# One MoE layer on one core: all expert low halves cut on VectorE, three shared units held back instead of two

## The reference

```python
x = x + jnp.tanh(g_xattn[0]) * attention(layernorm(x), ctx_1024, mask, W, b)
hidden = layernorm(x)
logits = hidden @ w_router
top_logits, top_idx = jax.lax.top_k(logits, 2)
scores = jax.nn.softmax(top_logits, axis=-1)
for e in range(8):                      # every token through its two experts
    proj, gate = jnp.split(rows_of_e @ fc1_w[e], 2, axis=-1)
    out_of_e = jax.nn.silu(proj) * gate @ fc2_w[e]
shared = jax.nn.silu(hidden @ gate_w) * (hidden @ up_w) @ down_w
x = x + jnp.tanh(g_ffn[0]) * (sum_of_two_experts_by_scores + shared)
```

## Time and profile before

| | |
|---|---|
| median of 3 runs | 239.54 us (239.11 to 240.22) |
| the profiled execution | 239.18 us |
| its span in the trace | 237.4 us |
| PE busy | 221.6 us, 93% |
| DVE busy | 173.8 us, 73% |
| ACT busy | 130.0 us, 55% |
| POOL busy | 125.4 us, 53% |
| PE's clock granted | 0.997 of full speed |

### The profile page before, as it was taken

One profiled execution on the slowest core, in us unless ns is written; L12 is line 12 of the kernel. 1 busy time (PEld: TensorE's weight loads), 2 busy tenths in 40 slices (PEclk: granted clock), 3 DMA queues, 4 the chain that ended last, 5 costly groups with the idle time before them and its releaser, 6 DMA issues.

```text
span 237.4 us, 5269 instructions
## 1 busy us (share of the span) xinstructions
PE 221.6 (93%) x1417; PEld 193.4 (81%) x1417; DVE 173.8 (73%) x514; ACT 130.0 (55%) x316; POOL 125.4 (53%) x177
## 2 busy tenths in 40 slices
PE   7988999999899999999599999999999999999980
PEld 7778899978688888888488888888888888887860
DVE  1978797797668899999967656656656656655895
ACT  2556888772647644555126556556556556555320
POOL 1698997564777877887601344344344343343600
PEclk9999999999999999999999999999999999999998
DMA  4899940000122215322242533433433432109777
GB/s 157 269 394 404 405 184 0 0 3 22 45 94 77 80 70 203 133 71 93 76 127 67 145 105 91 120 105 93 115 103 89 123 90 68 49 29 305 260 233 303
DMA packets 18131, 32.05 MB, mean 135 GB/s; under 512 B 3046, under 2 KB 9323, under 8 KB 18104
## 3 DMA queue, kind: packets, MB, share of 16 engines
q1 hardware_dynamic: 14096, 22.28, 29.6%
q0 software_dynamic: 3408, 8.46, 9.6%
q10 hardware_dynamic: 600, 0.97, 1.1%
HBM read 19.95 MB, written 12.67 MB: 137 GB/s over the span
## 4 chain that ended last, share of the span: by engine, by line
PE 45%; POOL 8%; issue 6%; DVE 3%; DMA 2%; ACT 0%; SPq 0%; DVEq 0%; POOLq 0%
PE bank L987 38%; POOL rows L388 6%; PE bank L1232 4%; PE bank L1252 4%; POOL ew_lo L243 2%; DVE acc L959 1%; DMA rows<-hrows,slot 1%; DMA hrows<-rows 1%; DVE act_lo L630 1%; DVE acc L702 1%; SPq L280 0%; DVE act L922 0%; ACT act_hi L443 0%; ACT act L581 0%; DVEq L62 0%
## 5 line engine op out<-in xcount | busy, mean ns | idle before, releaser
L430 POOL DMA_INDIRECT parts<-y_out,dst x39 | 38.8, 995 | 69.7 <-DVE dst L916 66.0
L922 DVE TENSOR_TENSOR act<-act,bank 128x256 f32<-128x256 f32 x39 | 16.4, 421 | 34.4 <-ACT act L581 32.6
L388 POOL DMA_INDIRECT rows<-hrows,slot x32 | 35.1, 1097 | 12.3 <-issue 12.1
L581 ACT ACTIVATE act<-bank 128x256 f32<-128x256 f32 x39 | 15.0, 384 | 37.5 <-PE bank L987 37.5
L987 PE MATMUL bank<-ew_hi,m_xt_hi 128*128 x78 | 30.9, 396 | 0.1
L987 PE MATMUL bank<-ew_hi,m_xt_lo 128*128 x78 | 30.8, 395 | 0.0
L987 PE MATMUL bank<-ew_lo,m_xt_hi 128*128 x78 | 30.7, 394 | 0.0
L987 PE MATMUL bank<-ew_hi,act_hi 128*128 x78 | 25.2, 323 | 0.2 <-DVE act_lo L630 0.2
L443 ACT ACTIVATE act_hi<-act 128x512 fp32r<-128x512 f32 x16 | 10.1, 631 | 21.8 <-DVE act L689 21.8
L987 PE MATMUL bank<-ew_hi,act_lo 128*128 x78 | 21.9, 281 | 0.0
L987 PE MATMUL bank<-ew_lo,act_hi 128*128 x78 | 21.9, 281 | 0.0
(11 more groups left out here) (182 smaller groups left out, 656.8 us busy)
## 6 DMA issues: line engine op xcount, KB each, us to landing
ew_raw<-in_chunks SPq DMA_DIRECT2D x12, 512.0 KB, 10.7
hrows<-rows SPq DMA_DIRECT2D x39, 130.0 KB, 2.3
low_buf<-parts SPq DMA_DIRECT2D x4, 512.0 KB, 4.2
high_buf<-parts SPq DMA_DIRECT2D x4, 512.0 KB, 5.1
acc<-in_x SPq DMA_DIRECT2D x7, 256.0 KB, 5.7
sw_raw<-in_chunks SPq DMA_DIRECT2D x3, 512.0 KB, 8.4
out<-acc SPq DMA_DIRECT2D x3, 512.0 KB, 3.4
rows<-pad_rows SPq DMA_DIRECT2D x9, 130.0 KB, 2.5
```

Source lines behind the costliest of these rows:

```text
L388: pool.indirect_dma_start(out=rows, out_offset=bass.IndirectOffsetOnAxis(ap=slot[:, h, k, i:i + 1], axis=0), in_=hrows[:, HT * h + i, :], ...
L430: pool.indirect_dma_start(out=parts, out_offset=bass.IndirectOffsetOnAxis(ap=dst[:, t:t + 1], axis=0), in_=y_out[:, t % SLOTS, :], in_offs ...
L581: a.activation(act[:, p, 0:I], M_H[p][:, 0:I], ACT.Silu).then_inc(s["m_sil"], 1)
L922: TT(act[:, p, 0:I], act[:, p, 0:I], M_H[p][:, I:2 * I], ALU.mult).then_inc(s["m_prod"], 1)
```

## The change

- All 23 low halves behind the first 7 are cut by DVE, by a new table `LATER` (1 with unit 0, 3 with unit 2, and so on up to 2 ahead of the product of unit 12). `MID` and `LAST` are gone, and POOL runs its scatters without cuts between or behind them.
- `HELD` is 3: the gate, up, product and down of unit 13 move behind the tiles. DVE's order in the tail has the third unit's `product` and `product_lo` between its high adds.
- ACT cuts four high halves earlier (ahead of `norm_second(6)`), one fewer in units 4 and 5 each, and none in a unit 12 of the loop, which is the last before the tiles now; the wait for the end of the attention (`mt_ps`) moves to chunk 12 (`FREE`).
- As the last unit ahead of the tiles is 12 in place of 13, the PSUM banks of the tile stage (`M_H`, `M_A`, `M_X`) are exchanged in pairs.

```diff
--- before.py
+++ after.py
@@ -44,11 +44,10 @@
 NH = 2
 HT = NT // NH
 IN_A = 7
-HELD = 2
+HELD = 3
 U0 = UNITS - HELD
-MID = tuple(IN_A + 2 * i for i in range(5))
-LAST = tuple(range(CHUNKS - 3, CHUNKS))
-LATER = {3: 1, 4: 1, 5: 1, 6: 1, 7: 1, 8: 1, 9: 2, 10: 2, 11: 2, 12: 3}
+FREE = SCH + 6
+LATER = {0: 1, 1: 0, 2: 3, 3: 1, 4: 2, 5: 1, 6: 1, 7: 1, 8: 3, 9: 2, 10: 3, 11: 3, 12: 2}
 ORDER = list(range(SCH + 8)) + list(range(SCH + 12, CHUNKS)) + list(range(SCH + 8, SCH + 12))
 
 
@@ -192,7 +191,7 @@
         GU = ((bank[0], bank[1]), (bank[2], bank[3]))
         BD = ((bank[4], bank[7]), (bank[5], bank[6]), (bank[4], bank[7]), (bank[5], bank[6]))
         BP = (bank[1], bank[7])
-        M_H, M_Y, M_A, M_X = (bank[2], bank[3]), (bank[4], bank[7]), bank[1], bank[0]
+        M_H, M_Y, M_A, M_X = (bank[0], bank[1]), (bank[4], bank[7]), bank[3], bank[2]
 
         names = """const_i const_c const_r const_m stats1 mean1 mean_first var_first rstd_first pre1 rstd1 xn_first xn_ready yp_ps yp_r tanh_g tg_half mask_b wr_h wr_l
             xt_ps xt_h xt_l wt_h wt_l y_h y_l xp_ps xp sc_ps sc_in sc_max sc_exp eT_ps eT_h eT_l mt_ps s_inv resid stats2 mean2 pre2 pow2 rstd2 h_ready
@@ -232,7 +231,7 @@
             return raw_[:, c, :], hi_[:, c, :], lo_[:, c, :]
 
         def by_pool(i):
-            return i < IN_A or i in MID + LAST
+            return i < IN_A
 
         def chunks_at(slot_):
             return 1 if 1 <= slot_ <= IN_A else 0
@@ -410,20 +409,9 @@
             rstd_second(NG - 2)
             scatter(0, 1, 3)
             rstd_second(NG - 1)
-            scatter(0, 3, 8)
-            cut_lo(pool, MID[0])
-            scatter(0, 8, 12)
-            cut_lo(pool, MID[1])
-            scatter(0, 12, 2 * HT)
-            cut_lo(pool, MID[2])
+            scatter(0, 3, 2 * HT)
             weight_fields(1)
-            scatter(1, 0, 6)
-            cut_lo(pool, MID[3])
-            scatter(1, 6, 11)
-            cut_lo(pool, MID[4])
-            scatter(1, 11, 2 * HT)
-            for i in LAST:
-                cut_lo(pool, i)
+            scatter(1, 0, 2 * HT)
             for t in range(N_TILES):
                 after(pool, "dst_f", t + 1)
                 after(pool, "y_sb", t + 1)
@@ -444,7 +432,7 @@
 
             def cut_hi(i):
                 a.wait_ge(chunk_in[i // 2], 16)
-                if i == IN_A:
+                if i == FREE:
                     after(a, "mt_ps", NG)
                 if i == CHUNKS - 4:
                     after(a, "tiles_known", 3)
@@ -548,6 +536,8 @@
             weight_tanh(0)
             silu(0)
             turn_h(NG - 3)
+            for i in range(IN_A, IN_A + 4):
+                cut_hi(i)
 
             norm_second(NG - 2)
             silu(1)
@@ -559,12 +549,12 @@
             silu(2)
             turn_h(NG - 1)
             silu_hi(2)
-            i = IN_A
+            i = IN_A + 4
             for n in range(3, U0 - 1):
                 if n == 5:
                     weight_tanh(1)
                 silu(n)
-                more = 3 if n < 6 else 2
+                more = 3 if n == 3 else 2
                 for j in range(i, i + more):
                     cut_hi(j)
                 i += more
@@ -781,11 +771,11 @@
                 v.tensor_copy(slot[:, h], slotf[:]).then_inc(s["slots"], 1)
 
             def cut_later(u):
-                mine = [i for i in range(IN_A, CHUNKS) if i not in MID + LAST]
+                mine = range(IN_A, CHUNKS)
                 first = sum(m for w, m in LATER.items() if w < u)
                 for i in mine[first:first + LATER.get(u, 0)]:
                     cut_lo(v, i)
-                    after(v, "chunk_lv", mine.index(i) + 1)
+                    after(v, "chunk_lv", i - IN_A + 1)
 
             turn_x(1)
             after(v, "mask_b", 1)
@@ -834,12 +824,14 @@
 
             residual(NG - 1)
             stats_second(NG - 1)
+            cut_later(0)
             product_lo(0)
             product(1)
             turn_h(NG - 2)
             product_lo(1)
             product(2)
             turn_h(NG - 1)
+            cut_later(2)
             product_lo(2)
 
             read_logits(1)
@@ -925,6 +917,7 @@
                 after(v, "aT_h", t + 1)
                 lo(act_lo[:, p, 0:I], M_A[:, 0:I], act_hi[:, p, 0:I], "aT_l")
 
+            cut_later(U0 - 1)
             product(U0 - 1)
             m_x(0, 0)
             product_lo(U0 - 1)
@@ -968,7 +961,9 @@
             add_high(0)
             product_lo(U0 + 1)
             add_high(1)
+            product(U0 + 2)
             add_high(2)
+            product_lo(U0 + 2)
             add_high(3)
             after(v, "done", NS)
             add_down(NS - 1)
@@ -1266,8 +1261,8 @@
             m_turn_x(0, 0)
             down(U0 - 2)
             m_turn_x(1, 1)
-            after(pe, "chunk_lp", IN_A + len(MID + LAST))
-            after(pe, "chunk_lv", CHUNKS - IN_A - len(MID + LAST))
+            after(pe, "chunk_lp", IN_A)
+            after(pe, "chunk_lv", CHUNKS - IN_A)
             after(pe, "sil", U0)
             after(pe, "tiles_known", 3)
             e = [expert_of(0)]
@@ -1299,7 +1294,9 @@
             after(pe, "m_prod", N_TILES)
             gate_up(U0 + 1)
             down(U0)
+            gate_up(U0 + 2)
             down(U0 + 1)
+            down(U0 + 2)
 
 
 def kernel(**inputs):
```

## The result

| | before | after |
|---|---|---|
| median | 239.87 us (239.11 to 240.22, 4 runs) | 248.03 us (245.69 to 249.22, 4 runs) |
| profiled execution | 239.18 us | 245.69 us |

The ratio is 1.033 (95% interval 1.025 to 1.042): the changed kernel is 8.2 us slower. I had forecast 235.5 us, with 238.0 as the upper end of the range. The forecast was wrong, in sign too. Ratios in this document leave out executions more than 1.5% above the fastest of their kernel; medians and ranges keep them.

A forecast was written before the change was run, and what follows sets the result against it. It took TensorE, busy 93%, as the bound except at its 2.3 us wait for the first expert tile and in the tail. 239.18 - 5.3 - 0.3 + 1.9 gave 235.5 us, range 234.2 to 238.0.

The forecast's parts named there:

- Scatters: POOL ahead of the tiles: removing five cuts between scatters saves 6.5 us, more DVE work costs 1.2 us back.
- first term: Start of the tiles' first transposition: from 117.24 to 111.95, -5.3 us, bounds -6.5 and -2.5.
- Moved unit: Ahead of the tiles: with three units held back, TensorE could start the first transposition at 110.72 at the earliest.
- Last scatter: End of POOL's last scatter: 107.5 us in place of 112.79, with the tile's transposition 4.45 us later.
- The 1.2 us that I charged: POOL's scatters slowed by eight more DVE cuts beside them, about 0.14 us each; bounds nothing and 4.0 us.
- rival 1: Scatters not slowed by more DVE work; TensorE bounds the first transposition at 110.72, time 234.3 us; chance 0.2.
- Low halves on DVE: Ahead of the first expert matmul: 15.6 us from unit 8's product to the last cut, done at 111.6; term 0.
- second term: Behind the first transposition: `down(11)` finds its `act_lo` ready, so TensorE's pause shrinks, -0.3 us.
- Tail: From `down(U0)` to the last `add_down`: the third held unit costs +1.9 us, bounds +1.7 and +2.4.
- Sum: Whole kernel: profiled 239.18 us - 5.3 - 0.3 + 1.9 = 235.5 us.
- The one on the other side: Scatters paced by their DMA queue, not POOL: transposition stays at 117.24, time 240.8 us; chance 0.05.
- Two engines in each other's way: Low-half cuts on DVE and POOL exclude each other: three DVE cuts took 5.85 us beside POOL's 3.76 us.

The follow-up runs named there:

- after_pause5: The changed kernel, with POOL filling an unused tile with 1000 zeros in the five places where cuts stood between scatters; 240.58 us, 1.000 of the kernel before.
- after_even: The changed kernel, with a POOL fill of 250 zeros behind each scatter from the fourth on; chip B, 241.56 us, 1.004 of the kernel before.
- after_narrow: The changed kernel, with scatters of 256-byte rows to another buffer, leaving out the experts' result; chip B, total time not comparable, TensorE not busy 0.00 us from 70 to 108.
- held3_mid5: The changed kernel, with five low halves cut by POOL between its scatters again, three units still held back; 242.95 us, 1.009 of the kernel before.
- hold2_behind3: The kernel before, with all 23 cuts on DVE and scatter n waiting until n - 3 has landed; chip C, 249.54 us, ratio 1.029.
- after_behind3: The changed kernel, with scatter n waiting until scatter n - 3 has landed; chip B, 237.88 us, 0.988 of the kernel before.
- even_again: The changed kernel with a POOL fill of 250 zeros behind each scatter from the fourth on, run again on chip C; 242.11 us, 1.008 of the kernel before.

## Why the prediction was wrong

**The step that failed** stands in its last lines: that TensorE is saturated between 60 and 110 us. I read that off and carried it into a kernel whose scatters follow 0.2 us closer. In **Scatters** I priced the five POOL cuts as 6.5 us of pure delay; "Nothing new holds the scatters" was true, but I never asked what the scatters hold. The prediction had TensorE starting to wait in that stretch only as a sign of being wrong, with no price. By the experiments the cuts were also the spacing that TensorE lived on: without them it stood for 6.00 of the 38 us from 70 to 108. The first term came out as +3.95 us (121.19 against 117.24) in place of -5.3.

The miss can be counted in units, against after_pause5, where units 5 and 6 start at 76.41 and 81.73, and units 9 to 12 at 94.31, 98.50, 102.70 and 106.89. Unit 5 took 84.80 - 76.08 = 8.72 for 5.32, unit 9 8.25 for 4.19, unit 10 5.91 for 4.20 (at the low clock: 0.77 us for a matmul of 0.39), unit 11 5.38 for 4.19 (0.92 of it for `act_lo`, as DVE was late). Together 10.4 us; 121.19 - 10.4 = 110.8, and the prediction had TensorE ready at 110.72.

**Moved unit**: right, by that number. **Last scatter**: predicted 107.5, measured 106.48 + 1.26 = 107.74. That is luck: the second half began 2.92 us late for `slot`, which waited for TensorE, and DVE stood still beside some scatters. The 1.2 us that I charged for more DVE work beside the scatters are not borne out. With 22 cuts on DVE between 64 and 112 us the 29 scatters have a mean of 1073 ns in after_pause5 and 1087 in after_even, against 1097 with 15 cuts before; in after_narrow, with 1066, the last one ends at 105.30, ahead even of rival 1's 106.3 (one execution, narrow rows). **Low halves on DVE**: the cuts are 0.687 us each, and from product(8) to the end of the last cut are 122.12 - 104.87 = 17.25 us, 1.37 of them a wait for a late `silu`: 15.9 against 15.6 worked out. The term of 0 was right for a chain that starts at 96; it started at 104.87, and held the first tile's `m_xt_lo` by some 0.7 us. So the **second term**, -0.3, came out as +0.42: the pause behind the first transposition did shrink, but the late DVE held the first tile. **Tail**: from `down(U0)` to the last `add_down` 241.38 - 231.57 = 9.81 us, against 234.88 - 227.20 = 7.68: +2.1 where I had +1.9, inside its bounds. The last high add indeed goes before `add_down`, as worked out. **Sum**: 239.18 + 3.95 + 2.13, and 0.42 from the first transposition to the tail (110.38 for 109.96 us), is 245.68; measured 245.69.

**Rivals.** The one on the other side had the scatters as its mechanism, but looked at their DMA queue and its landing. The queue did not pace POOL: 0.30 us stay between one scatter and the next. None had TensorE as the victim. No row of before could have shown it, since no row of scatters there was longer than six; but "what will now come at a higher rate, and who might feel it?" would have been a rival with a chance.

**Two engines in each other's way** stands, since cuts on DVE fell from 1036 to 687 ns when POOL's went, and rose to a mean of 844 in held3_mid5, where five came back.

## What to carry to other kernels

Work that sits between DMA issues on POOL may be their spacing. Before removing it, replace it by a fill of about the same length that reads nothing, and see whether anything else moves; then shorten the fill. And a gain that brings one engine to a point early is worth only what the next bound leaves: with three units held back TensorE waited 4.5 us and then paid in clock, with two it was the bound itself.

## What the runs showed of the hardware

- Indirect DMAs of 128 rows at a mean step of 1.29 to 1.37 us stop TensorE after 9 to 12 of them, without a semaphore wait. In the changed kernel that cost 2.5 us between 70 and 90 and 3.5 between 90 and 110; the worst of the other kernels lost 5.2 and 9.4. TensorE's signals to DVE come 3.5 to 4.8 us late, and SyncE's issues stretch from 8.95 to as much as 20.29 us for eight (hold2_behind3). At a mean of about 1.5 us TensorE lost 0.6 us or less. It came with rows of 256, 1024, 1040 and 1088 bytes alike.
- It is not the same on all chips: on B, after_narrow with 1.39 and 1.36 us lost nothing in its one execution, where the same kernel on C, with 1.35 and 1.30, lost 10.0. The changed kernel was not run on B.
- Through what it comes is open. Every time here, of all kernels, is that of an execution that was recorded, and traces of stalled kernels lack records: the row `rows<-pad_rows` of the page above has no landing time, where the kernel before has 2.5 us. The Trainium skill, "NOTIFIC — the notification-queue block", section "Overflow: three behaviours, one of which stalls the engine", says that the block which writes the records holds back its producers, rather than lose a record inside. That would fit a stop that depends on the number of events and not on bytes, and one that also reaches SyncE. No run here shows it, for none was made without a recording; and some kernels that did not stall lack the same records (after_pause5 among them). Whether the changed kernel is slower at all when nothing is recorded is therefore not shown.
- After 4.46 us without work TensorE's clock was granted at 0.50 for some 7 us; after 2.30 us in the profiled execution of the kernel before it stayed at 1.00. Waits of 4.33 to 5.83 us in after_behind3, after_even, even_again and held3_mid5 were followed by 0.50 as well.
